# Centred output weights, small normalisation work moved from GpSimd to VectorE, squares of two tiles summed by TensorE, and an order planned with other durations

## The reference, cut to what matters

```python
def attn(x, Wq1, Wq2, Wk1, Wk2, Wv, Wo, norm_w):
    q = silu(x @ Wq1 @ Wq2)
    f = sigmoid(x @ Wk1 @ Wk2)
    a = exp(log_sigmoid(f))
    h = scan over tokens of h = a * h + (1 - a) * (x @ Wv)
    out = q * h                                   # 512 features
    out = out * rsqrt(mean(out * out) + 1e-6) * norm_w
    return out @ Wo                               # back to 256 features
x = x + layernorm(attn(layernorm(x), ...))        # no gain, no bias
y = layernorm(x)
for i in range(6):
    y = gelu(y @ W1[i].T + B1[i]) @ W2[i].T + B2[i] + y     # 256 -> 1024 -> 256
    if i < 5: y = layernorm(y) * LN_G[i] + LN_B[i]
x = x + layernorm(y)
```

## Time and profile before

| | us |
|---|---|
| median of 3 runs (lowest, highest) | 656.39 (656.38, 657.34) |
| the profiled execution | 656.95 |
| its span, first to last instruction | 655.2 |
| PE busy | 637.2 (97%) |
| DVE, ACT, POOL busy | 448.2, 409.7, 284.2 |

### The profile page before, as it was taken

One profiled execution on the slowest core, in us unless ns is written; L12 is line 12 of the kernel. 1 busy time (PEld: TensorE's weight loads), 2 busy tenths in 40 slices (PEclk: granted clock), 3 DMA queues, 4 the chain that ended last, 5 costly groups with the idle time before them and its releaser, 6 DMA issues.

```text
span 655.2 us, 8823 instructions
## 1 busy us (share of the span) xinstructions
PE 637.2 (97%) x3015; PEld 530.1 (81%) x3015; DVE 448.2 (68%) x747; ACT 409.7 (63%) x678; POOL 284.2 (43%) x253
## 2 busy tenths in 40 slices
PE   7898999999999999999999999999999999999996
PEld 5677788888888888888888888888888888888886
DVE  6778665678567767758765777677687757764635
ACT  4988986788756555557555575555675545564433
POOL 6988442669516611338232175212372321222203
PEclk9999999999999999999999999999999999999999
DMA  8120000001101200003000021000020000000001
GB/s 283 66 97 1 1 1 1 1 1 66 65 0 48 82 1 2 0 1 117 13 2 0 1 64 66 1 1 1 0 66 1 0 2 0 2 1 32 33 1 66
DMA packets 8685, 19.36 MB, mean 30 GB/s; under 512 B 1600, under 2 KB 4672, under 8 KB 8640
## 3 DMA queue, kind: packets, MB, share of 16 engines
q1 hardware_dynamic: 8352, 18.53, 8.4%
q10 hardware_dynamic: 288, 0.26, 0.1%
HBM read 16.69 MB, written 2.10 MB: 29 GB/s over the span
## 4 chain that ended last, share of the span: by engine, by line
PE 89%; POOL 5%; issue 3%; DVE 1%; ACT 1%; DMA 0%; POOLq 0%; ACTq 0%; DVEq 0%
PE BK L457 43%; PE BK L742 39%; PE BK L566 2%; PE BK L752 2%; POOL WL L344 1%; POOL QB L551 1%; POOL SB L575 1%; PE BK L431 1%; PE BK L612 1%; PE BK L579 0%; POOL WL L298 0%; DMA X<-in_x 0%; PE BK L792 0%; PE BK L629 0%; ACT R L384 0%
## 5 line engine op out<-in xcount | busy, mean ns | idle before, releaser
L728 ACT ACTIVATE HH<-BK,B 128x512 fp32r<-128x512 f32 x192 | 132.4, 690 | 203.7 <-PE BK L457 203.3
L734 DVE TENSOR_TENSOR HL<-BK,HH 128x512 fp32r<-128x512 f32 x192 | 131.0, 684 | 82.6 <-ACT BK L731 82.2
L457 PE MATMUL BK<-XH,WL 128*128 128x512 f32 x416 | 163.7, 393 | 0.0
L457 PE MATMUL BK<-XH,WH 128*128 128x512 f32 x416 | 162.3, 390 | 0.0
L457 PE MATMUL BK<-XL,WH 128*128 128x512 f32 x416 | 162.0, 389 | 0.0
L742 PE MATMUL BK<-HH,WL 128*128 128x512 f32 x368 | 146.7, 399 | 0.0
L742 PE MATMUL BK<-HL,WH 128*128 128x512 f32 x368 | 143.7, 390 | 0.0
L742 PE MATMUL BK<-HH,WH 128*128 128x512 f32 x368 | 143.2, 389 | 0.0
L731 ACT ACTIVATE BK<-BK,B 128x512 f32<-128x512 f32 x192 | 125.6, 654 | 0.0
L457 PEld LDWEIGHTS BK<-XH,WH 128*128 128x128 f32 x416 | 78.1, 188 | 17.0
L457 PEld LDWEIGHTS BK<-XL,WH 128*128 128x128 f32 x416 | 78.2, 188 | 16.1
(11 more groups left out here) (121 smaller groups left out, 823.3 us busy)
## 6 DMA issues: line engine op xcount, KB each, us to landing
STG<-in_w SPq DMA_DIRECT2D x24, 512.0 KB, 3.7
out<-R SPq DMA_DIRECT2D x16, 128.0 KB, 1.9
X<-in_x SPq DMA_DIRECT2D x3, 512.0 KB, 7.8
R<-in_wv SPq DMA_DIRECT2D x1, 512.0 KB, 5.8
STG<-in_wo SPq DMA_DIRECT2D x1, 512.0 KB, 6.2
X<-in_x ACTq DMA_DIRECT2D x2, 128.0 KB, 3.0
X<-in_x SPq DMA_DIRECT2D x2, 128.0 KB, 2.8
R<-in_wq SPq DMA_DIRECT2D x1, 256.0 KB, 3.3
```

Source lines behind the costliest of these rows:

```text
L457: r = e.matmul(dst, s, m, start=first and i == 0, stop=last and i == len(todo) - 1)
L728: lambda e, ev=ev, hs=hs, bias=bias: e.activation(HH[:, hs, :], bank_of[ev][:, :], ACT.Gelu, bias=bias),
L734: lambda e, ev=ev, hs=hs: e.tensor_tensor(HL[:, hs, :], bank_of[ev][:, :], HH[:, hs, :].bitcast(f32), ALU.subtract), ("hlo", n, j))
```

## The change

Four edits. First, the output weights are centred: DVE sums each row of Wo over its 256 outputs (`wo_sum`), makes the negative mean (`wo_mean`) and adds it while it multiplies with the norm's weight (`wo_scaled`, 4 instructions), which POOL did before in one and without the mean. The projection's mean over features is then zero, so `l2` needs no mean: `l2_nm` on ACT and the addition on POOL become one DVE instruction per chunk (`x1`, straight from PSUM). Second, `_ve` and `_nb` move from POOL to DVE and `_ng` is gone. Third, for tiles 0 and 1 (`EAGER`) the three additions `ssum` on POOL are gone, and PE sums the squares of each `m` by itself into one PSUM bank: four groups of the matmuls of line 579 per tile (`rms0`, `rms1`, `rms2`, `rms`) in place of one. Fourth, the planner's durations are others, an engine is free a little before its instruction ends (`FREE`), and a signal takes 0.07 in place of 0.21.

```diff
+EAGER = 2
@@ the planner's table, one line of each
-         "_st": 0.41, "_mv": 0.15, "_nm": 0.42, "_rs": 1.03, "_ve": 0.2, "_ng": 0.2, "_nb": 0.2, "ms": 0.15,
+         "_st": 0.41, "_mv": 0.16, "_nm": 0.6, "_rs": 1.05, "_ve": 0.16, "_nb": 0.16, "ms": 0.16,
...
+FREE = {"sync": 0.0, "scalar": 0.11, "vector": 0.09, "gpsimd": 0.05, "tensor": 0.16}
-HOP = 0.21
+HOP = 0.07
@@ in arrange
-        clock[e] = t + (0.1 if done in moved else lasts(e, done))
+        spent = 0.45 if done in moved else lasts(e, done)
+        clock[e] = t + spent - FREE[e]
...
-            ends[done] = clock[e]
+            ends[done] = t + spent
@@ in sandwich, the output weights
-        op("gpsimd", -2, [("ldw_o",), ("nw",)],
-           lambda e: e.tensor_tensor(STG[:, 0, :].rearrange("p (m n) -> p m n", m=4),
-                                     STG[:, 0, :].rearrange("p (m n) -> p m n", m=4),
-                                     NW[:, :].unsqueeze(2).to_broadcast([128, 4, 256]), ALU.mult),
-           ("wo_scaled",))
-        split(0.5, raw["o"], WH[:, 1, 2560:3584], WL[:, 1, 2560:3584], "wo", [("wo_scaled",)])
+        op("vector", -3, [("ldw_o",), ("after", ("ulo", 0, 1))],
+           lambda e: e.tensor_reduce(WM[:, :], STG[:, 0, :].rearrange("p (m n) -> p m n", m=4),
+                                     mybir.AxisListType.X, ALU.add), ("wo_sum",))
+        op("vector", -2.9, [("wo_sum",)],
+           lambda e: e.tensor_scalar(WM[:, :], WM[:, :], -1 / 256, 1.0, ALU.mult, ALU.mult), ("wo_mean",))
+        for m in range(4):
+            op("vector", -2.8 + 0.1 * m, [("wo_mean",), ("nw",)],
+               lambda e, m=m: e.tensor_scalar(STG[:, 0, 256 * m:256 * m + 256], STG[:, 0, 256 * m:256 * m + 256],
+                                              WM[:, m:m + 1], NW[:, m:m + 1], ALU.add, ALU.mult), ("wo_scaled", m))
+        split(0.5, raw["o"], WH[:, 1, 2560:3584], WL[:, 1, 2560:3584], "wo", [("wo_scaled", m) for m in range(4)])
@@ in stats (both _ve operations go from "gpsimd" to "vector")
-            op("gpsimd", key + gap * 4 + 0.55, every,
-               lambda e: e.tensor_scalar(NM[:, t, :], MV[:, t, :, 0], -1.0, 1.0, ALU.mult, ALU.mult), (name + "_ng", t))
...
-            op("gpsimd", key + gap * 4 + 0.7, [(name + "_rs", t), (name + "_ng", t)],
-               lambda e: e.tensor_tensor(NBS[:, t, :], NM[:, t, :], RS[:, t, :], ALU.mult), (name + "_nb", t))
+            if name != "l2":
+                op("vector", key + gap * 4 + 0.7, [(name + "_rs", t), *every],
+                   lambda e: e.scalar_tensor_tensor(NBS[:, t, :], MV[:, t, :, 0], -1.0, RS[:, t, :], ALU.mult, ALU.mult),
+                   (name + "_nb", t))
@@ in sandwich, the loop over tiles (proj, and mm2 of n 2, wait for x1 in place of l2_nm)
-            for m in range(1, 4):
+            for m in range(1, 4) if t >= EAGER else ():
                 op("gpsimd", A + 2.0 + (LONG - 2) / 4 * m + 8.6,
                    [("osq", t, m), ("osq", t, 0) if m == 1 else ("ssum", t, m - 1)],
                    lambda e, m=m: e.tensor_tensor(SB[:, 0, :], SB[:, 0, :], SB[:, m, :], ALU.add), ("ssum", t, m))
...
-            product(Z, [("ssum", t, 3), ("one",)], rms, ("rms", t), ("ms", t))
+            if t >= EAGER:
+                product(Z, [("ssum", t, 3), ("one",)], rms, ("rms", t), ("ms", t))
+            for m in range(4) if t < EAGER else ():
+                def square(e, bank=None, m=m, t=t):
+                    for c in range(4):
+                        r = e.matmul((bank or bank_of["rms0", t])[:, c:c + 1], SB[:, m, c * 128:(c + 1) * 128], ONE[:, :],
+                                     start=(m == 0 and c == 0), stop=(m == 3), skip_group_check=True)
+                    return r
+                at, name = Z - 9 + 3 * m, ("rms", t) if m == 3 else (f"rms{m}", t)
+                if m == 0:
+                    product(at, [("osq", t, 0), ("one",)], square, name, ("ms", t))
+                else:
+                    op("tensor", at, [("osq", t, m), ("after", (f"rms{m - 1}", t))], square, name)
...
-            norm(Z + 4.5, "l2", t, R[:, t], p_of, 0.3, [("turned", k) if t == 0 else ("turn", "l1", t, k) for k in range(2)])
             for c in range(4):
-                op("gpsimd", Z + 5.5 + 0.6 * c, [("l2_nm", t, c)],
-                   lambda e, t=t, c=c: e.tensor_tensor(X[:, t, c, :], X[:, t, c, :], R[:, t, c, :], ALU.add),
-                   ("x1", t, c))
+                op("vector", Z + 4.5 + 0.4 * c, [("l2_rs", t), *x_in(c)],
+                   lambda e, t=t, c=c: e.scalar_tensor_tensor(X[:, t, c, :], p_of(c), RS[:, t, c:c + 1], X[:, t, c, :],
+                                                              ALU.mult, ALU.add), ("x1", t, c))
```

More of the change, by code:

```diff
@@ L151, in arrange @@
                 shut.add(w[1])
-        clock[e] = t + (0.1 if done in moved else lasts(e, done))
+        spent = 0.45 if done in moved else lasts(e, done)
+        clock[e] = t + spent - FREE[e]
         if done:
             issued.add(done)
-            ends[done] = clock[e]
+            ends[done] = t + spent
             if done in moved:
-                wire = max(wire, clock[e]) + moved[done] / RATE
+                wire = max(wire, t + spent) + moved[done] / RATE
                 ends[done] = wire + LAND
@@ L221, in sandwich @@
         MS = sb("MS", [128, NT, 4])
-        NM = sb("NM", [128, NT, 4])
+        WM = sb("WM", [128, 4])
         NBS = sb("NBS", [128, NT, 4])
@@ L288, in sandwich @@
         op("tensor", -100, [("idle_in",)], spin, ("spin",))
-        op("scalar", -98, [("one",)], lambda e: e.activation(WARM[:, :], ONE[:, :], ACT.Gelu), ("warm",))
+        op("scalar", -96.5, [("one",)], lambda e: e.activation(WARM[:, :], ONE[:, :], ACT.Gelu), ("warm",))
         def split(key, src, hi, lo, name, ready, hi_waits=(), lo_waits=(), lo_engine="gpsimd"):
@@ L569, in sandwich @@
                 op("tensor", M + 8.8, [("olo", t, m), ("ohi", t, m), ("wo_lo",)]
-                   + ([("after", ("proj", t, m - 1))] if m else [("l2_nm", t - 1, c) for c in range(4)] if t else []), proj, ("proj", t, m))
-            for m in range(1, 4):
+                   + ([("after", ("proj", t, m - 1))] if m else [("x1", t - 1, c) for c in range(4)] if t else []), proj, ("proj", t, m))
+            for m in range(1, 4) if t >= EAGER else ():
                 op("gpsimd", A + 2.0 + (LONG - 2) / 4 * m + 8.6,
@@ L598, in layer_norm @@
+            stats(Z + 6, "l3", t, x_of, lambda c, t=t: [("x1", t, c)], 0.4)
+            norm(Z + 9.5, "l3", t, R[:, t], x_of, 0.3, [("turned", k) if t == 0 else ("turn", "l1", t, k) for k in range(2)])
+            turn(Z + 11, "l3", t, [("l3_nm", t, c) for c in range(4)], ("mm1", t, 7))
         def layer_norm(E, n, b, t):
@@ L757, in sandwich @@
                     free = ([("claim", RING + i) for i in range(EARLY)] if n == 0 else
-                            [("l2_nm", NT - 1, c) for c in range(4)] if n == 2 else
+                            [("x1", NT - 1, c) for c in range(4)] if n == 2 else
                             [("y", max(n - 2, n // 2), k) for k in range(2)] if n < 4 * NB - 2 else
```

24 lines of the change are left out of this document (13 added, 11 removed).

## The result

| | median, us (lowest, highest) | executions |
|---|---|---|
| before | 656.47 (656.38, 657.34) | 4 |
| after | 663.21 (662.32, 663.91) | 4 |

The ratio is 1.0099, its 95% interval 1.0081 to 1.0116: **slower by 6.7 us**, where 654.1 and a range of 652.0 to 656.9 stood. The profiled execution took 663.64 us with a span of 661.4; 2.24 us lie around the span, 0.49 more than before.

A forecast was written before the change was run, and what follows sets the result against it. PE was taken as the bound, solid from 80 to 600 us, with stalls to win before. Stalls -11.1, squares +5.5 and remaining stalls +3.3 gave -2.3 us: 654.1 us from 656.39, range 652.0 to 656.9.

The forecast's parts named there:

- first projection behind `rms0`: Tile 0's first projection on PE, ready at 28.0, was to start behind the first group of squares at 28.2 us.
- the clock falls: Rival, chance 0.12: PE's clock drops after the wait at tile 0's first squares; 3.1 us lost for 6.54 us low.
- stay solid: PE was to have no new idle times between 80 and 600 us, so nothing was added there.
- The stalls won, -11.1: Six PE stalls before 80 us, 9.57 us idle plus 0.26 each, were all that the change could win: 11.1 us.
- the wait of 2.46 at tile 1's projection: PE's longest old stall, one of the six, was to go, with `x1` done near 51.8 for a projection at 53.4.
- The squares, +5.5: Six more groups of squares on PE for tiles 0 and 1, 0.91 us each, add 5.5 us of PE work.
- The chain to `rms0`, 27.4: Operations on DVE, ACT and POOL ahead of tile 0's first group of squares let it start near 27.4 us.
- 1 us lost: Rival, chance 0.23: DVE and POOL slow each other, PE stalls once or twice for 0.6 to 1 us; 655.1 to 656.2.
- 3.7 us nearly without streaming: At tile 0's first squares, 2.8 us idle plus a group of one-column matmuls, the stretch in which the clock might fall.
- wait of 2.8 us: PE's one remaining idle time over 1 us behind 13 us, near 24.6, ahead of tile 0's first group of squares.
- The covers of 0.6 us: `l3_nm` and an `olo` end 0.6 and 0.7 us before PE needs them near 60 us; breaking was a rival, chance 0.23.
- new stalls: Rival, chance 0.08: the order causes new stalls in tiles 2 and 3, 1 to 4 us; 655.1 to 658 us.

The follow-up runs named there:

- a_fill: Changed kernel with 20 unused matmuls of 512 columns behind tile 0's last product v, filling PE's wait ahead of the first group of squares; 662.47 us.
- a_hold: Changed kernel with POOL's first half piece of the feed-forward weights moved behind the second product o of tile 0; 662.99 us.
- a_odve: Changed kernel with the product o of tile 0 on DVE in place of POOL, planned anew; 661.42 us.
- b_late: Kernel before with PE summing the squares of tiles 0 and 1, tile 0's first group moved behind tile 1's second narrow product; 661.63 us.
- b_newtable: Kernel before with the fourth edit alone: planned with the new durations, signal time of 0.07 and early release; 668.41 us.
- b_centre: Kernel before with the first two edits alone, centred output weights and small operations on DVE, old durations, squares added on POOL; 661.82 us.
- c_sq: Changed kernel with tile 0's o on DVE and 8 unused matmuls behind tile 0's last product v; 660.05 us.

## Why the prediction was wrong

Its sum ended at a profiled 654.6; the profiled execution took 663.64. The 9.0 us between them:

| step of the prediction | forecast | measured | us |
|---|---|---|---|
| first projection behind `rms0` | 28.2 | 32.22 | +4.0 |
| "the clock falls", kept out of the sum | 0 | 8.27 - 5.63 between the first groups | +2.6 |
| 80 to 600 us "stay solid" | 0 | 1.05 | +1.0 |
| around the span | 0 | 2.24 - 1.75 | +0.5 |
| not assigned | | | +0.9 |

**The stalls won, -11.1: right, as far as is shown.** None of the six is over 1 us but the one that takes the place of two; `zq` starts at 13.54 (13.3), and the wait of 2.46 at tile 1's projection is gone. The 0.26 us that the sum adds to each stall were not measured by any run.

**The squares, +5.5: right.** 0.81 us a group where the clock is up. The reduction (1.21, taken 1.2), the scalings (1.38 for four) and `x1` (1.65 for four, taken 0.45 each) were sized well too.

**The chain to `rms0`, 27.4: the step that failed first.** It was right to 21.5 us. Then it gave `scan` 1.24 and the half piece 1.30 side by side, and these can't run side by side. The waiting adds 0.8 on the first scan, 1.1 on `_ve` and 1.0 on the second scan: 2.9 of the 3.0 us by which the group came late (30.39 against 27.4). The first projection came another 1.0 us later than the group, for `olo` waited beside the next half piece; a_fill, with the clock up, has this as well (31.81, 33.67). The text saw the sign, in the earlier trace rows, and took it for a mutual slowing worth "1 us lost", with a chance of 0.23 for any loss at all. The kernel before shows the rule in plain rows too, where POOL is the one that waits. Timelines of DVE and POOL of the kernel before:

```profile
21.97 1.32 DVE L548 TENSOR_TENSOR_SCAN SB<-AB,KB 128x512 f32<-128x512 f32 x1
24.48 1.19 DVE L548 TENSOR_TENSOR_SCAN SB<-AB,KB 128x512 f32<-128x512 f32 x1
```

```profile
22.30 0.98 POOL L371 TENSOR_SCALAR VE<-MV 128x4 f32<-128x4 f32 x1
23.36 0.20 POOL L374 TENSOR_SCALAR NM<-MV 128x4 f32<-128x4 f32 x1
...
24.61 1.05 POOL L379 TENSOR_TENSOR NBS<-NM,RS 128x4 f32<-128x4 f32 x1
```

An operation of 0.20 us takes 0.98 and ends at 23.28, the scan at 23.29; the next takes 1.05 and ends at 25.66, the scan at 25.67. A mean duration by shape hides that, its outliers show it. a_hold and a_odve bear it out from the other side: take one POOL instruction away and the next holds the scan up.

**The clock, chance 0.12: the step that failed second.** It was the rival on the slower side, priced at 3.1 us for 6.5 us at the lower level; it lasted 10.3 us, of which 7.6 had PE work in them, and cost 2.6 on the path. Against it stood that two waits of 1.5 us had done nothing. They did nothing in b_late either, but other waits of 1.95 (a_odve), 1.96 (b_newtable) and 2.46 us (b_centre) were followed by a fall: that a wait had been harmless once was weak evidence. The text had counted "3.7 us nearly without streaming", and gave it too little weight. With a right wait of 2.8 us the clock would probably have been lost too; then the sum would have come near 657 (an estimate: 654.6 and the 2.6 of the table). The start of the program, which spoke for the case, has a catch: its matmuls run at half pace (0.43 us each), but the windows list the granted clock there as 1.00, so this row shows a pace and not a granted clock. The Trainium skill ("TensorE: Matmul & The Clock Gate", section on what's actually happening) has the array throttled by default and activity releasing it; the runs agree, as the clock stayed up through the wait where an unused stream of matmuls filled it, in a_fill and c_sq.

**The other rivals.** The covers of 0.6 us held: `x1` is done at 59.6 for a projection at 60.14 (a cover of 0.5, as a scan of tile 1 took 2.23 for the same reason as above), and no wait over 1 us stands at the `l3` transposes. No wait got shorter than forecast.

**80 to 600 us.** The list of PE's waits names one line in this stage:

```profile
PE BK L635 <- DVE P L632: 1.0, 4, 0.3
```

Four waits of `mu`. They come with the new durations, as the kernels planned with either table show; which entry of the table makes them was not tried. The prediction had new stalls as a rival of chance 0.08 and left them out of the sum.

**What stays open.** 0.9 us are not assigned; 0.2 of it are idle times from 38 to 80 us. Why 0.2 to 0.7 us more lie around the span is open as well: they are there in every execution of every kernel with centred weights (1.98 to 2.48) and in none of the others (1.75 to 1.84). Repairing the two steps that failed does not bring the forecast about: c_sq has the first projection at 28.57 and the clock at 1.00 to 80 us, and its profiled execution of 658.70 is still 4.1 us above 654.6. Of these 1.0 us is PE's idle time from 80 to 600, 1.2 are its waits at 36.8, 43.1 and 55.5, 0.4 the start of the projection, 0.35 lie around the span, and 1.2 are not assigned. No version faster than before came out: the best two lie 3 us above it.
